# Splitting the queries of a graph-attention pass into bf16 parts, and making its one-hot matrices in bf16

## The reference

```python
for l in range(2):
    xn = _layernorm(h, ln1_g[l], ln1_b[l])
    q = (xn @ wq[l] + bq[l]).reshape(n, 8, 32)        # k and v likewise
    scores = einsum('ehd,ehd->eh', q[dst], k[src]) / sqrt(32)
    m = segment_max(scores, dst); ex = exp(scores - m[dst])
    agg = segment_sum(ex / z[dst] * v[src], dst)
    h = h + agg @ wo[l] + bo[l]
    h = h + gelu(layernorm(h) @ w1[l] + b1[l]) @ w2[l] + b2[l]
```

## Time and profile before

| | us |
|---|---|
| median of 3 executions (lowest, highest) | 5669.54 (5665.43, 5674.77) |
| the profiled execution | 5669.54 |
| its span | 5668.4 |
| PE, PE weight loads busy | 4086.4, 3165.1 |
| DVE, ACT, POOL busy | 2726.6, 1629.8, 3662.6 |

### The profile page before, as it was taken

One profiled execution on the slowest core, in us unless ns is written; L12 is line 12 of the kernel. 1 busy time (PEld: TensorE's weight loads), 2 busy tenths in 40 slices (PEclk: granted clock), 3 DMA queues, 4 the chain that ended last, 5 costly groups with the idle time before them and its releaser, 6 DMA issues.

```text
span 5668.4 us, 64573 instructions
## 1 busy us (share of the span) xinstructions
PE 4086.4 (72%) x18103; PEld 3165.1 (56%) x18103; DVE 2726.6 (48%) x6258; ACT 1629.8 (29%) x4708; POOL 3662.6 (65%) x3085
## 2 busy tenths in 40 slices
PE   4444444667964444599794777669999999978886
PEld 3332233445653222366463555558888888867775
DVE  6365558886435444888532666671000001134445
ACT  1111113663321111577231222220000000046564
POOL 4466667888885666888887555578888800056663
PEclk9776667998987666799896888889999999978997
DMA  7688886763258888576423555546666655456664
GB/s 257 195 285 283 285 280 152 161 160 49 22 126 270 279 281 291 130 167 139 76 14 64 146 147 148 146 84 139 153 142 141 148 152 150 143 153 177 174 177 129
DMA packets 719528, 937.58 MB, mean 165 GB/s; under 512 B 275269, under 2 KB 510836, under 8 KB 719048
## 3 DMA queue, kind: packets, MB, share of 16 engines
q1 hardware_dynamic: 404210, 524.56, 31.0%
q0 software_dynamic: 298192, 385.84, 29.3%
q10 hardware_dynamic: 16774, 23.00, 1.1%
HBM read 713.40 MB, written 219.69 MB: 165 GB/s over the span
## 4 chain that ended last, share of the span: by engine, by line
PE 33%; issue 23%; POOL 15%; DVE 11%; another core or an unknown queue 8%; DMA 6%; SPq 3%; DVEq 1%; ACT 0%; POOLq 0%; ACTq 0%
PE bank L2371 19%; POOL sc L865 6%; POOL ATT L879 6%; PE bank L2464 6%; PE bank L2461 3%; POOL arena L842 3%; DVE arena L1326 3%; DMA ATT<-arena 3%; DMA sc<-arena 3%; SPq L568 2%; DVE arena L1236 2%; DVE arena L1599 2%; PE bank L2356 1%; DVE arena L1307 1%
## 5 line engine op out<-in xcount | busy, mean ns | idle before, releaser
L842 POOL DMA_INDIRECT arena<-KVT,arena x832 | 802.1, 964 | 483.6 <-issue 267.3
L2371 PE MATMUL bank<-arena 128*128 128x256 f32 x5000 | 1101.3, 380 | 1.7 <-DVE arena L1656 1.2
L2209 PE MATMUL bank<-arena 128*128 x1664 | 579.4, 503 | 686.8 <-issue 455.9
L2371 PEld LDWEIGHTS bank<-arena 128*128 128x128 f32 x5000 | 946.8, 190 | 129.6 <-DVE arena L1656 2.0
L2209 PEld LDWEIGHTS bank<-arena 128*128 128x128 f32 x1664 | 382.3, 244 | 883.2 <-issue 815.4
L842 POOL DMA_INDIRECT arena<-YT,arena x416 | 405.8, 975 | 674.1 <-DMA YT<-arena 456.0
L895 POOL DMA_INDIRECT arena<-ATTR,arena x416 | 655.0, 1574 | 145.0 <-issue 145.0
L879 POOL DMA_INDIRECT ATT<-arena x391 | 643.7, 1646 | 125.3 <-issue 109.4
L865 POOL DMA_INDIRECT sc<-arena x391 | 641.7, 1641 | 123.8 <-issue 110.0
L842 POOL DMA_INDIRECT arena<-X1T,arena x416 | 396.9, 954 | 282.8 <-DVE arena L1599 151.5
L1326 DVE TENSOR_TENSOR arena<-arena,bank 128x256 f32<-128x256 f32 x832 | 297.9, 413 | 568.0 <-remote 392.0
(11 more groups left out here) (305 smaller groups left out, 5482.0 us busy)
## 6 DMA issues: line engine op xcount, KB each, us to landing
VE<-arena SPq DMA_DIRECT2D x208, 512.0 KB
arena<-VE SPq DMA_DIRECT2D x208, 512.0 KB
arena<-ATT SPq DMA_DIRECT2D x250, 320.0 KB
arena<-AM SPq DMA_DIRECT2D x250, 320.0 KB
ATT<-arena POOLq DMA_DIRECT2D x25, 1600.0 KB, 6.5
arena<-ATT SPq DMA_DIRECT2D x75, 384.0 KB
arena<-LOCT SPq DMA_DIRECT2D x208, 128.0 KB
AM<-arena SPq DMA_DIRECT2D x100, 256.0 KB
```

Source lines behind the costliest of these rows:

```text
L842: GP.indirect_dma_start(out=ring[:, i % n, k, :], out_offset=None, in_=table, in_offset=bass.IndirectOffsetOnAxis(ap=idx[:, 4 * i + k:4 * ...
L2209: mm = P.matmul(b_[:, 0:264], OHQ[:, i % 3, k * 128:(k + 1) * 128], Q[:, bass.ds(ws[k], 1), :], start=True, stop=True)
L2371: mm = P.matmul(bank[j][:, 0:256], left[:, 128 * j:128 * (j + 1)], right[:, u, :], start=(u == 0), stop=(u == W - 1))
```

## The change

`Q` (float32) becomes three bf16 parts: `Q3[..., 0, :]` is q rounded to bf16, `Q3[..., 1, :]` the rounded rest, `QL` what is left then. ACT and DVE now write q and the self scores to `QWA`, which has room for ten windows. After every fifth window DVE runs `split`: four instructions over 5 x 264 values, each waiting for the one before. `q_split` counts these, and POOL, SP and PE wait for its fifth step at the start of a pass instead of for the last `self_made`; ACT waits for the split of the windows whose room it writes again. The one-hots of the k passes are made in bf16, and PE multiplies each by the three parts in turn, adding up in one bank.

```diff
+    Q3 = view(o_q, W, 2, 132).bitcast(BF)
+    QL = view(o_acc, W, 132).bitcast(BF)
+    QWA = view(o_wv, 10, 264)
...
-            SY.wait_ge(*self_made(f"qkv{l}", W))
+            SY.wait_ge(*q_split(f"qkv{l}", 5))
...
-            GP.wait_ge(*self_made(f"qkv{l}", W))
+            GP.wait_ge(*q_split(f"qkv{l}", 5))
...
+        def split(name, w0, w1_):
+            q_ = QWA[:, w0 % 10:w0 % 10 + 5, :]
+            V.wait_ge(*self_made(name, w1_))
+            d.then(V.tensor_copy(Q3[:, w0:w1_, 0, :], q_))
+            d.then(V.tensor_tensor(q_, q_, Q3[:, w0:w1_, 0, :], ALU.subtract))
+            d.then(V.tensor_copy(Q3[:, w0:w1_, 1, :], q_))
+            V.tensor_tensor(QL[:, w0:w1_, :], q_, Q3[:, w0:w1_, 1, :], ALU.subtract).then_inc(q_split.sem, 1)
...
-            V.tensor_reduce(Q[:, w, 256:264], ...).then_inc(self_made.sem, 1)
+            V.tensor_reduce(QWA[:, w % 10, 256:264], ...).then_inc(self_made.sem, 1)
+            if w % 5 == 4:
+                split(name, w - 4, w + 1)
...
-                V.tensor_scalar(OHQ[:, i % 3, :], PLACES[:, i % 6, :], pcol, None, ALU.is_equal).then_inc(onehot.sem, 1)
+                V.tensor_scalar(OHT[:, i % 3, :], PLACES[:, i % 6, :], pcol, None, ALU.is_equal).then_inc(onehot.sem, 1)
...
-            S.activation(Q[:, u, 0:256], ...)
+            if u // 5 >= 2:
+                S.wait_ge(*q_split(name, u // 5 - 1))
+            S.activation(QWA[:, u % 10, 0:256], ...)
...
-            P.wait_ge(*self_made(f"qkv{l}", W))
+            P.wait_ge(*q_split(f"qkv{l}", 5))
...
-                    mm = P.matmul(b_[:, 0:264], OHQ[:, i % 3, k * 128:(k + 1) * 128], Q[:, bass.ds(ws[k], 1), :],
-                                  start=True, stop=True)
+                    lhs = OHT[:, i % 3, k * 128:(k + 1) * 128]
+                    P.matmul(b_[:, 0:264], lhs, Q3[:, bass.ds(ws[k], 1), 0, :], start=True, stop=False)
+                    P.matmul(b_[:, 0:264], lhs, Q3[:, bass.ds(ws[k], 1), 1, :], start=False, stop=False)
+                    mm = P.matmul(b_[:, 0:264], lhs, QL[:, bass.ds(ws[k], 1), :], start=False, stop=True)
```

More of the change, by code:

```diff
@@ L246, in program @@
     OUTB = view(o_ring, 2, 768)
-    Q = view(o_q, W, 264)
-    OHQ = view(o_acc, 3, 512)
+    Q3 = view(o_q, W, 2, 132).bitcast(BF)
+    QL = view(o_acc, W, 132).bitcast(BF)
+    QWA = view(o_wv, 10, 264)
     D8 = view(o_S, SB, 16, 8)
@@ L359, in program @@
     self_made = Signal(nc, "self_made", qkv0=W, qkv1=W)
+    q_split = Signal(nc, "q_split", qkv0=5, qkv1=5)
     scan_in = Signal(nc, "scan_in", flags=1, w0=7, w1=7)
@@ L1139, in normed @@
             return V.tensor_scalar(dst, src, MS[:, 2 * w:2 * w + 1], RS[:, w:w + 1], ALU.subtract, ALU.mult)
+        def split(name, w0, w1_):
[5 more added lines that the diff above has]
+            V.tensor_tensor(QL[:, w0:w1_, :], q_, Q3[:, w0:w1_, 1, :], ALU.subtract).then_inc(q_split.sem, 1)
         def self_scores(name, w, o):
             V.wait_ge(*q_scaled(name, w + 1))
-            d.then(V.tensor_tensor(o[:, 0:256], Q[:, w, 0:256], o[:, 256:512], ALU.mult))
-            V.tensor_reduce(Q[:, w, 256:264], o[:, 0:256].rearrange("p (h d) -> p h d", d=32), AX,
+            d.then(V.tensor_tensor(o[:, 0:256], QWA[:, w % 10, 0:256], o[:, 256:512], ALU.mult))
+            V.tensor_reduce(QWA[:, w % 10, 256:264], o[:, 0:256].rearrange("p (h d) -> p h d", d=32), AX,
                             ALU.add).then_inc(self_made.sem, 1)
+            if w % 5 == 4:
+                split(name, w - 4, w + 1)
         def load_and_project():
@@ L1757, in scale_query @@
         def scale_query(name, u, o):
-            S.activation(Q[:, u, 0:256], o[:, 0:256], ACT.Copy, scale=float(1.0 / np.sqrt(32.0))).then_inc(q_scaled.sem, 1)
+            if u // 5 >= 2:
+                S.wait_ge(*q_split(name, u // 5 - 1))
+            S.activation(QWA[:, u % 10, 0:256], o[:, 0:256], ACT.Copy, scale=float(1.0 / np.sqrt(32.0))).then_inc(q_scaled.sem, 1)
         def keep_rows(name, u, o):
```

## The result

The kernel after takes 5721.6 us (median of 4 runs, 5715.7 to 5727.0) against 5670.5 before (5665.4 to 5674.8): ratio 1.009, 95% interval 1.0073 to 1.0108. That is 51 us more, slower as predicted, but 24 us above the upper end of the range. The profiled execution took 5725.35 us with a span of 5724.2, 55.8 more than before's.

A forecast was written before the change was run, and what follows sets the result against it. POOL's queue carries most of the chain, its k passes set by gathers in flight and their landing. Nothing in qkv0, k0 and k1, +15.9 us at k1's start: 5669.5 + 15.9 = 5685.4 us, range 5667 to 5698.

The forecast's parts named there:

- Pace of the k passes: k0 and k1: set by gathers in flight and their landing, not DVE or PE; 626 us each, cost 0.
- PE, 12 short matmuls, 3 us a group: k passes: 12 shorter matmuls replace 8 a group, 3 us a group, hidden because PE works two groups ahead; cost 0.
- third rival: k passes: bf16 matmuls with an address each no shorter than float32 halves, 6.04 us a group; 83 us more, 5768; chance 0.05.
- One-hots: k passes on DVE: 208 bf16 one-hots save 0.15 us each, 31 us, worth 0 on the path.
- The split: DVE: four dependent instructions over 1320 values with three gaps, S = 6.23 us; 4.9 if casts are fast, kept for the range.
- qkv0: Five splits, 31 us, hidden by DVE's 42.60 us wait for a DMA; cost 0.
- mix0: Splits delay windows 4, 9 and 14 by 7.0, 6.3 and 5.8 us, 19 by 0; window 24's split adds 6.2.
- high end: Start of k1: delays of 9.7, 7.1, 6.2 and 6.3 us, last split ending at 1675.4, k1 19.9 us later.
- GpSimd's scatters: mix0: two-input split instructions block scatters, which end 0 to 15 us later, by 1670.5 at most, hidden behind the last split.
- First rival: Same mechanism but small: casts fast, or DVE and ACT regain most of the split; +8.4 us, 5677.9; chance 0.26.
- Second rival: k passes shorten because DVE's pace decides when POOL's ring is free; 52 us saved less the 15.9, 5633; chance 0.09.
- Sum: Nothing in qkv0, k0 and k1, +15.9 us at the start of k1, passed on by POOL's later queue; 5685.4.

The follow-up runs named there:

- two_parts_third: Kernel after with two of the three query parts multiplied, the third made and left out: 5649 us against 5641 for the kernel before, ratio 1.0017.
- splits_only: Kernel before with five splits a layer added into unused memory without gaps, k passes still float32: 5653 us against 5643 for the kernel before, ratio 1.0020.
- after_third: Kernel after, unchanged, rerun on a chip of the faster kind: 5246 us against 5234 for the kernel before, ratio 1.0023.
- one_part_again: Kernel after with one bf16 matmul a chunk, the two other query parts made but left out: 5608 us against 5641 for the kernel before, ratio 0.9944.

## Why the prediction was wrong, point by point

- **Pace of the k passes, "landing of the gathers hides it": wrong, and the step that failed.** Expected 626 us each and 0; measured +20.0 and +10.8, and +16.5 and +20.8 in a second pair. The landing of rows was not all that DVE waited for: of its 568 us of idle time, most of which I put down to DMA, 306 stood where only PE's signal is awaited. And on this kind of chip instructions added to PE's queue lengthen the pass whatever they do (nine waits a chunk: 86 and 90 us). The sign I had excluded exists too: with one matmul a chunk before's passes lose 24 to 29 us. My evidence, two passes of equal length with unequal DVE work, was an average over a swing. It said nothing on PE, whose load was the same in both.
- **PE, 12 short matmuls, 3 us a group:** the matmuls are as short as assumed, one every 0.13 to 0.22 us. I counted matmuls and their time, not what stands on PE's queue. It went from 23 to 39 records a group, 8 more register operations among them; the third rival came near with "an address each", but priced it by the matmul's duration. In the slow stretches a chunk takes 4.2 us. DVE waits for PE in some groups, not in every one as that rival's sign had it, and it did so before the change.
- **One-hots:** 0.34 us instead of 0.48, worth nothing, as said. two_parts_third, with them, has before's passes.
- **The split:** S predicted 6.23, measured 6.26 (1690.03 to 1696.29). The other end of the range was real as well: a cast into rows without gaps took 0.848 us, predicted 0.85. That it depends on the gaps agrees with the Trainium skill, "Vector Engine (DVE) Microarchitecture Reference", section 5.1, read as in the prediction.
- **qkv0:** hidden, k0 starts at 261.9 as before at 262.2.
- **mix0:** predicted 19.1 before the last split, measured 24.2 (the last scores come 43.9 later, k0 ends 19.7 later). Scores of window 4 to 7: +8.3 for 7.0; 9 to 11: +7.1 for 6.3; 14 to 15: +5.7 for 5.8; 19: 0 for 0. The rest, 3.1, comes in windows to which I gave nothing (11 to 14 and 15 to 19). k1 starts 21.9 later behind the end of k0, above the high end of 19.9. The mechanism was right and mis-sized by 6.0 us.
- **GpSimd's scatters:** they ended at 1683.7 and were hidden behind the last split, as said.
- **First rival** (8.4): its condition, quick casts, is met by splits_only, and k1 starts 10.1 us late there behind the end of k0 (7.0 in all). **Second rival:** wrong cause, right place. The passes can be shortened from the compute side, by less on PE's queue. **Sum:** 15.9 predicted; 21.9 and, unexpected, 19.7 and 10.8 came.

The Trainium skill speaks against Theory A: "ifetch is hidden by the ~20-cyc/instr NX issue floor" ("Runtime: NRT & Kernel Launch", section "Instruction fetch mechanics"). On kind II the traces agree, with no register operation over 0.3 us. On kind I the instructions of 0.70 us would, if it were the fetch that makes them slow, which no run shows; the transfers of instructions themselves look alike on both, blocks of 16 KB that took 0.9 to 1.4 us in k0 of after and 0.9 to 1.1 in after_third, and a fetch does not explain a late signal of work already done.

What stays open is the mechanism. Shown is that instructions taken off PE's queue or added to it shorten or lengthen the k passes on kind I, and not on kind II. Not shown is why. Theory A, a queue that gets its instructions too slowly, explains neither the slow operations at 15 records nor the signals that come late, by 17 us in the case shown, those of DVE as well. Something that delays queues and signals together would, and one candidate is untested: every time on record comes with a span and a granted clock of its own, so from an execution that was traced, and what is counted here as records is what a trace keeps. The traces of the unchanged kernel after hold 51 to 52 thousand updates of semaphores on kind I and 91 thousand on kind II, so on kind I many were not kept. No run tells whether the loss, or the difference between the kinds, is there without tracing, and no chip was seen to be of both kinds. The count orders the runs on kind I only roughly: 598 us a pass at 15 records, 619 and 624 at 27 and 25, 641 at 39, but 681 at 34 and 710 at 42 with the nine waits.

## What to carry to other kernels

Before splitting one matmul into several with addresses in registers, count the instructions that its queue gets for each step of the pipeline, not only their busy time, and look in the trace at the longest register operation. Before calling idle time a wait for DMA, look up which signals the waiting instruction names, and when the work behind each was done. Cut a pipeline that waits for transfers into its stretches before saying what hides what: an average share of busy time hid a swing in which compute was the bound half of the time. A cast is worth laying out without gaps.

## What the runs showed of the hardware

- On chips of kind I single instructions of PE's queue, register operations and waits alike, took 0.70 us for 15 to 20 us on end, and matmuls without any wait stood 1.0 us. On kind II, at the same count and with the DMA engines fuller, no register operation did.
- On kind I signals came long after the work: PE's by 12.8 us (matmul ended at 284.50, DVE went on at 297.29, before) and 17.4 us (343.20, 360.60, after), DVE's own by 5.6 us (one_part_again). Before third chunks, where only PE's signal is awaited, DVE stood 117 to 241 us a pass in before and after, and 0.9 us or less in every run on kind II.
- Nine waits on semaphores that had long been reached cost 0.21 us a chunk on kind I (88 us a pass of 416 chunks), and nothing on chips of kind II.
- The same shape, 128 x 1320 bfloat16 out of float32, took 1.528 us into rows with gaps and 0.848 without; a float32 copy of that size without gaps 0.848, a subtraction 1.53.
